# Whole-matrix weight transfers, and two products of the next sequence placed between output tiles

## What is computed

```python
r = sigmoid(x @ Wr.T); k = x @ Wk.T; v = x @ Wv.T
state = cumsum(k * v / clip(scale, 1e-10), axis=time) * scale    # scale = exp(pos * log sigmoid(decay))
out = r * state
normed = (out - mean) * rsqrt(var + eps) * gn_weight + gn_bias   # mean, var over the whole sequence
attention = normed @ Wo.T
# experts, for each of 64: tokens that picked it (at most 64 of them)
g = silu(x_e @ w_gate); u = x_e @ w_up; y = (g * u) @ w_down     # 512 -> 384 -> 512
combined[tok] += y * weight                                       # plus silu(x@sg) * (x@su) @ sd
```

## Time and profile before

| | us |
|---|---|
| median of 3 runs | 727.75 (726.48 to 728.10) |
| the profiled execution | 726.94 |
| its span | 725.1 |
| TensorE busy (PE) | 677.6 (93%) |
| VectorE busy (DVE) | 331.1 (46%) |
| GpSimd busy (POOL) | 218.7 (30%) |
| weight and other loads (queue 1) | 169.25 MB, 61.5% of 16 engines |
| weight transfers | 384 of 384 KB |

### The profile page before, as it was taken

How to read it: one execution, slowest core, us unless ns; L and a number is a source line. 1 busy time by engine, 2 the same in 40 slices (tenths; PEclk the granted TensorE clock), 3 DMA queues, 4 the chain that set the end, 5 groups by cost and what they waited for, 6 DMA issues and landing times.

```text
span 725.1 us, 9207 instructions
## 1 busy us (share of the span) xinstructions
PE 677.6 (93%) x3229; PEld 408.0 (56%) x3229; DVE 331.1 (46%) x809; ACT 160.9 (22%) x259; POOL 218.7 (30%) x209
## 2 busy tenths in 40 slices
PE   3999999899999998999999999999999999997883
PEld 2587878688788754445545545554554554543330
DVE  5887567648987781323323323323323323322121
ACT  4822215523111411112112112112112112111110
POOL 4637456326546322021211220212221221112101
PEclk9999999689999999999999999999999999999997
DMA  9101016700866899499999999999999999999992
GB/s 322 63 13 47 1 30 234 243 31 1 298 242 257 301 338 310 153 366 378 392 390 376 348 392 376 391 349 381 386 390 377 355 384 376 392 357 380 380 349 33
DMA packets 79996, 202.69 MB, mean 280 GB/s; under 512 B 10403, under 2 KB 10531, under 8 KB 79568
## 3 DMA queue, kind: packets, MB, share of 16 engines
q1 hardware_dynamic: 64160, 169.25, 61.5%
q0 software_dynamic: 8928, 21.33, 12.3%
q10 hardware_dynamic: 6864, 11.54, 4.3%
HBM read 178.66 MB, written 23.59 MB: 279 GB/s over the span
## 4 chain that ended last, share of the span: by engine, by line
PE 67%; SPq 11%; DVE 8%; issue 2%; DMA 2%; POOL 1%; ACT 1%; ACTq 0%; DVEq 0%; POOLq 0%
PE bank L1560 18%; PE bank L1348 12%; SPq L246 11%; PE bank L1581 9%; PE bank L1481 8%; PE bank L1500 5%; PE bank L1370 4%; DMA w_sb<-in_L_ffn_w_up 2%; PE bank L1395 2%; PE bank L1508 2%; PE bank L1568 1%; DVE key L1059 1%; DVE best L1058 1%; PE bank L1471 1%; DVE state L970 1%
## 5 line engine op out<-in xcount | busy, mean ns | idle before, releaser
L618 POOL DMA_INDIRECT out_dram<-ym,midx x32 | 51.3, 1602 | 313.9 <-DVE ym L1245 198.7
L1560 PE MATMUL bank<-w_sb,xT 128*64 128x384 f32 x768 | 131.2, 494 | 6.9 <-DMA w_sb<-in_L_ffn_w_up 4.3
L1348 PE MATMUL bank<-x_hi,w_parts 128*128 128x512 f32 x384 | 121.8, 399 | 5.3 <-DVE x_lo L954 3.4
L1581 PE MATMUL bank<-w_sb,guT 128*64 128x512 f32 x384 | 90.0, 604 | 4.5 <-issue 4.5
L1560 PEld LDWEIGHTS bank<-w_sb,xT 128*64 128x64 f32 x768 | 53.5, 137 | 71.1 <-issue 59.5
L1348 PEld LDWEIGHTS bank<-x_hi,w_parts 128*128 128x128 f32 x384 | 73.5, 192 | 22.9 <-DVE x_lo L954 4.2
L1185 DVE TENSOR_TENSOR gu<-sg,bank 128x384 f32<-128x384 f32 x32 | 17.7, 554 | 126.9 <-issue 119.8
L1348 PE MATMUL bank<-x_lo,w_parts 128*128 128x512 f32 x192 | 75.1, 400 | 0.0
L1481 PE MATMUL bank<-sh_sb,xS 128*128 128x384 f32 x192 | 63.9, 486 | 0.0
L1581 PEld LDWEIGHTS bank<-w_sb,guT 128*64 128x64 f32 x384 | 28.4, 140 | 54.9 <-issue 54.9
L1481 PEld LDWEIGHTS bank<-sh_sb,xS 128*128 128x128 f32 x192 | 35.7, 191 | 22.3
(11 more groups left out here) (180 smaller groups left out, 948.8 us busy)
## 6 DMA issues: line engine op xcount, KB each, us to landing
w_sb<-in_L_ffn_w_down SPq DMA_DIRECT2D x128, 384.0 KB, 11.8
w_sb<-in_L_ffn_w_gate SPq DMA_DIRECT2D x96, 384.0 KB, 12.1
w_sb<-in_L_ffn_w_up SPq DMA_DIRECT2D x96, 384.0 KB, 12.4
extra<-in_L_ffn_w_gate SPq DMA_DIRECT2D x32, 384.0 KB, 12.4
extra<-in_L_ffn_w_up SPq DMA_DIRECT2D x32, 384.0 KB, 12.2
ring<-in_L_attn_x SPq DMA_DIRECT2D x14, 256.0 KB, 3.8
xt_dram<-xwT ACTq DMA_DIRECT2D x12, 256.0 KB, 3.4
xS<-xt_dram SPq DMA_DIRECT2D x12, 256.0 KB, 13.4
```

Of the source, the lines that this page charges most:

```text
L618: pool.indirect_dma_start(out=out[:, :], out_offset=bass.IndirectOffsetOnAxis(ap=midx[j % 3][u][:, :], axis=0), in_=ym[u][:, :], in_offset ...
L1348: ins = pe.matmul(ps[u][:, :], w, xp, start=(n == 0), stop=(n == len(parts) - 1))
L1560: ins = pe.matmul(ps[e * C:(e + 1) * C, 0:I], xT[:, c, e * C:(e + 1) * C], gate_up(2 * j + u, e, k)[:, c, :], start=(c == 0), stop=(c == K ...
L1581: ins = pe.matmul(pair_bank(j, u)[e * C:(e + 1) * C, :], guT[0][:, c, e * C:(e + 1) * C], down(2 * j + u, e)[:, c, :], start=(c == 0), sto ...
```

## The change

PIECES becomes 1: each matrix of an expert is one transfer of 768 KB with rows of 6144 bytes, and there are 192 weight transfers. FILL follows, 32 in place of 64. A new function `first_of_second` makes the products r and v of step 8, in halves of six matmuls each, in tiles 4 to 7 of the loop of sequence 0: r in 4 and 5, v in 6 and 7. Step 8 then makes k alone. It waits for 7 of the 8 logit copies; the wait for the last one and for the last residual moves to step 9.

```diff
--- before.py
+++ after.py
@@ -48,7 +48,7 @@
 GROUPS = E // 4
 W = KC * I
 SLOTS = 3
-PIECES = 2
+PIECES = 1
 FILL = 2 * PIECES * 16
 ADD = 16
 LEAD = 4
@@ -1322,15 +1322,36 @@
                                         start=(c == 0), stop=(c == KC - 1))
                     ins.then_inc(rows_ready, 1)
 
+            def first_of_second(i, half):
+
+                if half == 0:
+                    pe.wait_ge(xlo_ready, TILES + TILES // 2)
+                    pe.wait_ge(x2_done, KC + 1 + i)
+                    need(pe, (sig_done, vcopy_done)[i], STEPS - 1)
+                parts = []
+                for k in range(KC):
+                    hi, lo = w_hi[i][:, 0, k, :], w_lo[i][:, 0, k, :]
+                    parts += [(hi, x_hi[0][:, k, :]), (hi, x_lo[0][:, k, :]), (lo, x_hi[0][:, k, :])]
+                size = len(parts) // 2
+                for n in range(half * size, (half + 1) * size):
+                    w, xp = parts[n]
+                    ins = pe.matmul((ps_r, ps_v)[i][0][:, :], w, xp, start=(n == 0), stop=(n == 2 * size - 1))
+                if half:
+                    ins.then_inc((r_ready, v_ready)[i], 1)
+
             def step(s):
                 u, c, h = s % 2, s % KC, s % STEPS // KC
                 if s == STEPS:
+                    pe.wait_ge(logit_copied, TILES - 1)
+                if s == STEPS + 1:
                     pe.wait_ge(x2_done, TILES)
                     pe.wait_ge(logit_copied, TILES)
                 if s % STEPS in (0, KC):
                     pe.wait_ge(xlo_ready, s // STEPS * TILES + (h + 1) * TILES // 2)
                 for i, (ps, free, ready) in enumerate(((ps_r, sig_done, r_ready), (ps_v, vcopy_done, v_ready),
                                                        (ps_k, kv_done, k_ready))):
+                    if s == STEPS and i < 2:
+                        continue
                     if s == 0:
                         pe.wait_ge(hi_ready, i + 1)
                     need(pe, free, s - 1)
@@ -1443,6 +1464,8 @@
                     project(i + 4)
                 if i:
                     router(i - 1)
+                if i >= KC:
+                    first_of_second((i - KC) // 2, i % 2)
                 turn_xw(i)
                 if i + 1 < TILES:
                     turn_x(TILES + 1 + i)
```

## The result

The changed kernel takes 718.19 us (median of 4 runs, 714.33 to 719.5) where the kernel before takes 727.42 beside it: a ratio of 0.9865 [0.9823, 0.9907], 1.3% faster. The forecast was 712.7. The profiled execution took 719.23 us with a span of 717.4, so its span fell by 7.7 us and not by 14.2; it was one of the two longer executions of the four. Run again on another occasion the same kernel had a median of 716.41.

A forecast was written before the change was run, and what follows sets the result against it. The weight stream was taken to bound the experts, and GpSimd's adds the tail after the change. Moved products (8.5 us) start the adds earlier; paced at 9.7 us they end the span 14.2 us sooner: 726.9 - 14.2 = 712.7 us, range 706.5 to 721.

The forecast's parts named there:

- What bounds it, and the clock: Expert stretch: weight stream at 14.66 us a pair is slower than TensorE's 13.68; tile loop's clock stays at 1.00.
- rival (d): Tile loop: the clock still falls near 132 us, so the moved products gain 0; 721.2 us, chance 0.07.
- Part 1, 8.5 us: Moving 24 products of r and v into the tile loop brings the expert phase 8.5 us earlier.
- Takes 4.7 us beside a weight transfer: 147.0: Start of step 8: last turned-tile store, issued at 142.3, lands at 147.0; VectorE begins near 149.6 instead of 155.48.
- Goes on without a wait worth the name: Sequence 1: VectorE starts 5.9 us earlier, catches up a 2.43 us wait before 171.74, gaining 8.3, then hardly waits.
- TensorE waits for VectorE's eight rounds already: Behind step 13 TensorE already waits for VectorE's rounds; used to support the 8.5 us gain from the moved products.
- Part 2, the stream: Expert weights: longer rows save 0.40 us a pair, 10.5 us in all; last down product near 687.5, 21 us earlier.
- The sign that I had named for it: SP's weight issues should show a pitch near 14.3 us; 14.66 would mean the stream gained nothing.
- The adds decide: Tail: GpSimd's scatter-adds set the end, each landing under load 1.0 us slower, 9.7 us an add; span ends at 710.9.
- Rival (a): Tail: adds do not slow down, staying at 8.67 us; 18.2 us less, 708.7 us, chance 0.2.
- (b): Tail: load on the adds doubles, 2.1 us each and more for shared tiles; 6.4 less, 720.5 us, chance 0.13.
- Rival (c): Weight stream gains nothing from longer rows, leaving only the moved products' 8.5 us; 718.4 us, chance 0.08.

The follow-up runs named there:

- experiment 2: Changed kernel with PIECES back at 2, so only the moved r and v products remain; 720.65 us, ratio 0.9911 to the kernel before.
- Experiment 4: Changed kernel with most 768 KB pair transfers carrying half the columns of both experts, in rows of 3072 bytes; 722.13 us, ratio 0.9931.
- experiment 1: Kernel before with PIECES = 1 alone, so one transfer per matrix and no moved products; 720.03 us, ratio 0.9891.
- experiment 3: Two runs on the changed kernel: TensorE's product moving the rounds' result one step later, 711.67 us; the w_down transfer beside the store moved later, 711.58 us.
- later turn of experiment 3: Changed kernel with TensorE's product that moves the rounds' result behind step 14, not 13, and VectorE's merging behind it; 711.67 us, ratio 0.979.
- late load of experiment 3: Changed kernel with the single w_down transfer issued at 142.25 us moved behind the shared weights, at about 172 us; 711.58 us, ratio 0.9777.

## Why the prediction was right and wrong

**What bounds it, and the clock: right.** Before, the stream was slower than TensorE; the moved products kept the clock at 1.00 in the tile loop, and so rival (d) falls. k began at 143.63, where the step had 142.8.

**Part 1, 8.5 us: right alone in one execution (6.9 by the medians), wrong beside part 2.** This is the step that failed. "Takes 4.7 us beside a weight transfer: 147.0" took the landing from the trace of before, although the weight transfer beside it is itself one that part 2 turns from two pieces into one. By the DMA rows the store took 5.2 to 6.8 us in six executions with the one piece beside it and the moved products; with two pieces 4.0, with nothing beside it 2.0 to 4.6 in three. The second mistake was the size of what hangs on it. "Goes on without a wait worth the name" holds for VectorE, but the 2.43 us that I counted as caught up did not last: it was 4.6 us ahead at step 10 (167.16 for 171.74) and 3.3 at the turn of the rounds. Five of its products with r took 1.28 to 1.61 us (one did before, the others took 0.69), while GpSimd multiplied at the same time. And "TensorE waits for VectorE's eight rounds already" was true but was used the wrong way round: TensorE is done 8.8 us earlier there (194.40 - 6.38 = 188.02 for 197.66 - 0.86 = 196.80) and VectorE 3.3, so a wait of 0.86 us becomes one of 6.38, and behind it the clock drops. In experiment 2, where VectorE was 9.2 us ahead at that place, the wait stayed at 0.85.

**Part 2, the stream: right, a little large.** I had the last down product at 687.5, which is 12.7 us less than the 8.5 of part 1 alone would give; against the front it came 11.1 us earlier (431.6 to 420.4 us behind the first expert product). In the window from 600 to 640 all traffic rose from 385 GB/s to 394, or 2.3%, and to 393 to 399 over the nine kernels with long rows, where the two rows read of before gave 3.6%. Over the whole run queue 1 took 61.5% of 725.1 us before and 59.6% of 717.4 after for the same 169.2 MB, 4.1% less. Experiment 4 shows that the row is the cause, as the step had it.

The sign that I had named for it did not show: SP issues w_down of pair 11 at 408.53 and of pair 28 at 639.95, 13.6 us a pair and not 14.3. That is TensorE's pitch, and SP waits for TensorE's down products all along; its waits from 400 to 700 us, before and after:

```profile
SPq L246 <- PE bank L1581: 2.4, 1, 2.4
...
SPq L246 <- PE bank L1604: 143.0, 20, 12.0
```

The DMA engines are full all the same (share 1.03 to 1.04 from 400 to 640), so the issues no longer show the stream's pitch. The bytes do: from 410 to 640 us queue 1 moved 75.64 MB before and 78.05 after. At 4.85 MB a pair (4.72 of weights and half a tile of 256 KB) I estimate 14.7 us a pair before and 14.3 after, 0.45 less where I had 0.40. So the stream did stay the slower of the two, as forecast. Why SP comes to wait for buffers while the engines stay full was not tested.

The last down product came 1.6 us less early than that. One clause of the tail failed beside it, "none of these landings holds TensorE for over 1 us": before the down product at 669.20 TensorE waited 1.62 us for VectorE's copy to ym, which the landing of an add had released at 668.37. TensorE was idle for 3.8 us from 630 to the last down product, where the sign said under 3.

**The adds decide: right, by terms of the wrong shape.** I gave each of six landings 1.0 us. Single adds rose by 0.7 to 0.8 (8.67 to 9.4 and 9.5), the batch by 3.4 (13.03 to 16.41), the add with the gathers behind it hardly (9.46 to 9.53), and the two intervals behind the stream's end were 5.7 and 6.2 where I had 6.6. From (12,0) to the end I had 84.9 us, and it was 84.0. One price for all landings was only right in the sum; that the batch pays more because it is longer (13.0 us of transfer against 7.1) is my reading, and no run took its size by itself. Rival (a) had 80.9 us for that stretch and (b) 92.7, so the measured one lies nearer to (a). The Trainium skill, DMA: Bandwidth & Descriptors (Queues, rings and completion order), says that an engine alternates between queues only at packet borders; the direction agrees with the batch at the three row lengths here (11.9, 13.0 and 16.4 us). The doubling that (b) took from it does not hold for a single add (0.7 us, not 2.1), while the batch, 16.4 us, even passes the 15.3 that (b) gave it.

**Rival (c) falls** by experiment 1: 7.0 us from part 2 alone. The same page's some 358 GB/s for the HBM side of a core (Where 436 GB/s comes from) is passed in the window from 600 to 640 by all traffic together at every row length run here, 365 to 399 GB/s; queue 1, with the weights, has 334 to 363 of it.

The sum against the execution: forecast 14.2, of which part 1 carried 8.5 and gave 1.1, the tail 5.7 and gave 6.6. Part 1 fell 7.4 us short and the tail gave 0.9 more; that the tail came so near is in part luck, since the errors of its single adds cancel.

**Open.** Why the store lands later beside one piece than beside two of the same bytes wasn't settled. By the DMA rows it landed, in experiment 1 with the order of before, in 4.9 us beside one piece; with nothing beside it, it took anything from 2.0 to 4.6. So the transfer is part of the delay, not all of it. That the low clock from 192 to 205 follows from the wait and not from something else rests on the thirteen executions of the table: the seven with a wait of 0 to 0.86 us kept 1.00 from 180 to 205, the six with 1.72 to 6.38 us had a mean of 0.93 to 0.86. No run changed the clock alone.

## What to carry to other kernels

When a change has two parts, look whether one of them alters a transfer that stands beside the wait on which the other's gain hangs; take the parts apart first, since their sum alone hides that they take from each other. A duration under contention read from before is only good for after if its neighbour is unchanged. And when an engine is made early, ask who it then waits for, and whether it falls to a lower clock there: putting its own work ahead of that wait was worth as much as an earlier store (both in experiment 3).

## What I had not expected of the hardware

For the stream the length of a row mattered, and the size of a transfer did not: 768 KB in rows of 3072 bytes ran as 384 KB did (rest 448.6 and 448.7 us). Rows of 1536 bytes, in transfers of 192 KB, made the kernel 3.3% slower. The price is paid by the small queue beside it: three tiles of accumulation took 11.9, 13.0 to 13.2 and 16.1 to 16.4 us beside rows of 1536, 3072 and 6144 bytes, and 8.2 and 8.4 behind the stream's end. VectorE's product of 128x512 with r took up to 1.61 us beside GpSimd's work in the changed kernel (1.80 with the later turn of experiment 3) where it takes 0.69 alone. And TensorE's clock fell to half for some 3 us after a wait of no more than 1.72 us (late load of experiment 3: 0.50 from 191 to 193).
